# A new plan of the forty slots in the attention and expert phase of one core

## The chip, the core and the metric

The kernel runs on one NeuronCore of a Trainium2 chip, with 16 DMA engines of its own. The metric is the device time of one execution in microseconds. Five engines work side by side, each through its own instruction list in order: TensorE (PE in the profile), VectorE (DVE), ScalarE (ACT), GpSimd (POOL) and SyncE (SP), which here issues all plain transfers. They meet only at semaphores: an instruction whose semaphore isn't there yet holds all that stands behind it on its engine.

## The reference

The input is x (8, 512, 128) and runs through two stages, in float32:

- x + layernorm(A(layernorm(x))), where A is a bidirectional selective state-space layer. The change doesn't touch it.
- x + layernorm(F(layernorm(x))), where F has causal attention with 16 query heads and 4 key/value heads of size 8, rotary embedding, RMS norms, a residual (x2), and a mixture of 8 experts (top 2 of a softmax router; each expert computes w2 (silu(w1 h) * (w3 h)) with 256 hidden columns, weighted by the router), again with a residual.

## The kernel before

The second stage (`ffn_phase`) begins at 1052 us. It handles the 8 batch entries of 512 tokens as a software pipeline. A period b = -2 ... 10 has forty slots t = 0 ... 39, and every engine has a function (`pe_period`, `act_period`, `dve_period`, `pool_period`) whose loop over t writes its instructions out in the order of the slots; nothing plans this at run time. SyncE's `sp_period` is one list per period, without slots. In period b there are at work:

- *front*, batch b+2: layer norm and RMS norm (`dve_in` 0 to 3, with `pool_in_rstd` between 1 and 2; `h` and `hn` are the two results), transpose, projections of q, k, v (`pe_proj` 0 to 3), the rotary products (`dve_rope`) and their sums (`pool_add` 0 for `qf`, 1 for `kf`). q and k are then split into three bf16 parts: `act_part` and `pool_part` in turns, 0 and 1 for q, 2 and 3 for k.
- *att + 1*, batch b+1: the parts go to memory (`sp_parts_out`) and come back spread over partitions, one group of 4 heads at a time (`sp_parts_in` 0 to 3: three q transfers and one k transfer); TensorE computes scores for the row maxima (`pe_max`, from slot 14 on, group g needs its fetch at slots 14, 24, 34 and 4 of the next period), VectorE reduces them (`dve_max`), and `pe_nm`, `act_nm`, `dve_nm`, `sp_max` bring the negative maxima into q's rows.
- *att*, batch b: one tile of scores per slot. TensorE (`pe_st`) fills one of two PSUM buffers, ScalarE takes the exponential twice (`act_exp`, to f16 and to f32), GpSimd computes the rest of the f16 rounding (`pool_split`), and TensorE multiplies by v four slots later (`pe_pv`). After each ten slots a group is done: `act_den` copies the denominators, `dve_og` adds the three parts; both stand ahead of that slot's exponential and maxima.
- *post*, batch b-1: reciprocals of the denominators and the product (`dve_og_fin`, one per slot in slots 5 to 8), output projection (`pe_wo`), residual `x2` (`dve_post`), RMS norm, router (`pe_gate`, 27 steps `dve_gate` at the slots of `GATE_AT`, `pe_count`), and `pool_scatter` in 8 indirect DMAs of tokens into slots by expert (xs).
- *moe*, batch b-2: experts. 15 tiles of 128 tokens in 4 groups q; each group has 5 steps at every other slot (`moe_at`): transpose of `xg`, first product and tanh, second product and gating (twice), and `pe_down`, `act_y` (the copy to `ysb`) and `sp_y` (its store) behind. `sp_w` loads the weights of the expert that each tile belongs to, four tiles of 384 KB at a time, into 8 buffers.
- *end*, batch b-3: `pool_gather` (8 indirect DMAs), weighted sum (`dve_end`), layer norm, output.

TensorE's two buffers for scores let it run at most two tiles ahead of the exponentials (L1303, `exp_done`); the exponential waits for the product with v of six tiles before; `pe_xg` waits for the whole `xg` transfer, `pe_a` for the group's four weights; the first `pool_gather` waits for the stores of all four groups.

## Time and profile before

| | |
|---|---|
| median of 3 runs | 2045.14 us (2045.09 to 2046.9) |
| the profiled execution | 2054.69 us, its span 2052.8 us |
| TensorE busy | 1401.5 us (68%) |
| VectorE busy | 1617.2 us (79%) |
| ScalarE busy | 1134.1 us (55%) |
| GpSimd busy | 1380.8 us (67%) |

The rows below come from that one execution. "Busy" is time inside instructions; a gap in front of an instruction is put down to what released it. L1549 is line 1549 of the kernel; lines are those of the functions above. The span starts at 0; the second stage fills 1052 to 2052.8 us. A period's slot is told here by its first exponential (L1549); the first of batch 4 starts at 1496.66 us.

### The profile page before, as it was taken

How to read it: one execution, taken by the hardware profiler on the slowest of the kernel's cores; microseconds unless marked ns; L12 is line 12 of the kernel's file. 1: busy time of each engine (PE TensorE's matmuls, PEld its weight loads, DVE VectorE, ACT ScalarE, POOL GpSimd, SP SyncE). 2: the span in 40 equal slices, each digit the busy share in tenths (PEclk: the TensorE clock that was granted, in tenths of full speed). 3: DMA queues.
4: the chain of work that ended last, by engine and by line, in shares of the span. 5: the costliest groups of instructions: out<-in, count | busy, mean ns of one | idle time of the engine just before them, and what ended most of it. 6: DMA issues, size and time to landing. Idle time of an engine off the chain costs nothing. (4 is left out here: it accounts for less than half of the span.)

```text
span 2052.8 us, 28868 instructions
## 1 busy us (share of the span) xinstructions
PE 1401.5 (68%) x8048; PEld 986.7 (48%) x8048; DVE 1617.2 (79%) x2570; ACT 1134.1 (55%) x1901; POOL 1380.8 (67%) x1225
## 2 busy tenths in 40 slices
PE   3776666775767767567635877787777787878553
PEld 1444444454534545445422444555555555656453
DVE  2999999999999999999924567586868686866432
ACT  4555665555656545666301877666565666667110
POOL 1776777777777766777742777768686867778333
PEclk9777778887778877778555898899989988999776
DMA  4201222202122102222011112435343524343453
GB/s 161 88 30 55 103 83 103 83 19 85 83 103 83 77 26 83 103 83 98 1 43 43 38 47 79 129 94 153 95 125 97 146 93 139 102 135 117 123 165 93
DMA packets 113886, 184.93 MB, mean 90 GB/s; under 512 B 9856, under 2 KB 86656, under 8 KB 109440
## 3 DMA queue, kind: packets, MB, share of 16 engines
q1 hardware_dynamic: 109664, 175.14, 25.2%
q0 software_dynamic: 4096, 8.40, 1.4%
q8 instruction: 44, 0.72, 0.2%
q14 instruction: 82, 0.67, 0.1%
HBM read 153.03 MB, written 25.89 MB: 87 GB/s over the span
## 5 line engine op out<-in xcount | busy, mean ns | idle before, releaser
L731 POOL TENSOR_TENSOR hc<-hb,cb 128x512 f32<-128x512 f32 x512 | 654.7, 1297 | 247.7 <-DVE hb L610 213.9
L610 DVE TENSOR_TENSOR_SCAN hb<-da,dbu 128x512 f32<-128x512 f32 x512 | 599.9, 1203 | 5.6 <-DVE stats L635 4.0
L499 ACT ACTIVATE da<-dt,a_neg 128x512 f32<-128x512 f32 x512 | 352.2, 718 | 354.8 <-DVE hb L610 303.7
L2041 POOL TENSOR_TENSOR pp<-pt,pp 128x512 f16<-128x512 f32 x320 | 379.0, 1188 | 169.3 <-ACT pt L1550 167.1
L331 PE MATMUL yp<-ident,hc 128*128 128x128 f32 x2048 | 357.9, 317 | 64.9 <-POOL hc L731 64.4
L1689 DVE TENSOR_REDUCE mx<-ms 128x1 f32<-128x384 f32 (+3 forms) x352 | 220.2, 636 | 206.3 <-PE ms L1273 199.4
L331 PEld LDWEIGHTS yp<-ident,hc 128*128 128x128 f32 x2048 | 297.3, 165 | 174.5 <-POOL hc L731 93.9
L603 DVE TENSOR_TENSOR dbu<-dtu,bp 128x512 f32<-128x512 f32 x512 | 324.0, 678 | 2.9 <-PE bp L319 2.2
L1549 ACT ACTIVATE pp<-scores,lift 128x512 f16<-128x512 f32 x320 | 220.3, 688 | 133.4 <-PE scores L1309 128.8
L319 PE MATMUL bp<-st,sel 96*128 96x512 bf16 x256 | 116.7, 456 | 154.3 <-DVE dbu L603 151.7
L1550 ACT ACTIVATE pt<-scores,lift 128x512 f32<-128x512 f32 x320 | 220.3, 688 | 0.0
L1328 PE MATMUL og<-pp,vpad 128*128 128x512 f16 (+3 forms) x1024 | 205.8, 322 | 10.2 <-DVE osum L1710 5.6
L285 PE MATMUL wp<-xpad,wu 128*128 128x512 f32 x256 | 136.8, 627 | 22.8 <-ACT xpad L429 15.4
L1273 PE MATMUL ms<-k,q 72*128 72x384 bf16 (+3 forms) x512 | 139.7, 331 | 0.0
L1328 PEld LDWEIGHTS og<-pp,vpad 128*128 128x128 bf16 x1024 | 105.0, 105 | 66.2 <-issue 26.4
L1309 PE MATMUL scores<-q,k 75*128 75x512 bf16 (+3 forms) x512 | 132.0, 320 | 0.0
L1270 PE MATMUL ms<-mask,identb 128*128 128x128 bf16 (+2 forms) x352 | 93.3, 265 | 49.0 <-issue 17.3
L319 PEld LDWEIGHTS bp<-st,sel 96*128 96x128 bf16 x256 | 25.7, 101 | 210.1 <-DVE dbu L603 188.8
L2060 POOL DMA_INDIRECT yk<-ys_scratch,pos_e x64 | 61.8, 966 | 66.3 <-DMA ys_scratch<-ysb 51.8
L1306 PE MATMUL scores<-mask,identb 128*128 128x256 bf16 (+1 forms) x320 | 85.5, 267 | 25.9 <-ACT pt L1550 24.5
L1394 PE MATMUL pa<-xt,wt 128*128 128x128 f32 x480 | 73.6, 299 | 36.1 <-DVE ga L1845 34.0
L1566 ACT ACTIVATE th<-pa 128x512 f32<-128x512 f32 (+1 forms) x64 | 36.4, 569 | 109.3 <-PE pa L1387 91.1
(193 smaller groups left out, 2351.8 us busy)
## 6 DMA issues: line engine op xcount, KB each, us to landing
cb<-c_scratch SPq DMA_DIRECT2D x16, 3072.0 KB, 11.9
wt<-ffn_w_e SPq DMA_DIRECT2D x120, 384.0 KB, 3.9
cb<-c_scratch SPq DMA_DIRECT2D x16, 1024.0 KB, 4.6
q<-q_scratch SPq DMA_DIRECT2D x96, 96.0 KB
xg<-xs_scratch SPq DMA_DIRECT2D x8, 960.0 KB, 5.6
ys_scratch<-ysb SPq DMA_DIRECT2D x24, 256.0 KB, 2.3
q_scratch<-qp SPq DMA_DIRECT2D x24, 128.0 KB
k<-k_scratch SPq DMA_DIRECT2D x32, 72.0 KB
```

Of the source, the lines that this page charges most:

```text
L319: nc.tensor.matmul(bp[:, n % 2, :], sel[:, n, :], st[:, d, :], start=True, stop=True).then_inc(b_ready, 1)
L331: last = nc.tensor.matmul(yp[:, c, h * P:(h + 1) * P], src[:, c * P:(c + 1) * P], ident[:, :], is_transpose=True, start=(s < 0 and h == 0 ...
L499: nc.scalar.activation(da[:, s % NDA, :], dt[:, d, h, :], ACT.Exp, scale=a_neg[:, d, h, n:n + 1]).then_inc(da_done, 1)
L603: nc.vector.tensor_tensor(dbu[:, s % 2, :], dtu[:, d, h, :], bp[:, n % 2, :], ALU.mult).then_inc(dbu_done, 1)
L610: nc.vector.tensor_tensor_scan(hb[:, s % NHB, :], da[:, s % NDA, :], dbu[:, s % 2, :], 0.0, ALU.mult, ALU.add).then_inc(scan_done, 1)
L731: nc.gpsimd.tensor_tensor(hc[:, s % NHC, :], hb[:, s % NHB, :], cb[:, d, s // 2, :], ALU.mult).then_inc(hc_done, 1)
L1273: last = nc.tensor.matmul(heads[:, i, :], q9[0:PART_ROWS, h0_ + i, c * P:(c + 1) * P], k9[0:PART_ROWS, (h0_ + i) // 4, 0:width], start=Fal ...
L1328: last = nc.tensor.matmul(og[:, kc * P:], vpad[:, kc, h, :], pp[:, (ST_TILES * b + t) % NPR, part, at:at + SEQ - kc * P], start=first, sto ...
L1549: nc.scalar.activation(pp[:, (ST_TILES * b + t) % NPR, 0, 0:width], scores_in, ACT.Exp, bias=lift[:, :], scale=SCALE)
L1550: nc.scalar.activation(pt[:, (ST_TILES * b + t) % NPR, 0:width], scores_in, ACT.Exp, bias=lift[:, :], scale=SCALE).then_inc(exp_done, 1)
L1689: nc.vector.reduce_max(mx[:, c, h:h + n], ms[:, t % 2, 0:n * (c + 1) * P].rearrange("p (n k) -> p n k", n=n), mybir.AxisListType.X).then_i ...
L2041: nc.gpsimd.tensor_tensor(pp[:, (ST_TILES * b + t) % NPR, 1, 0:width], pt[:, (ST_TILES * b + t) % NPR, 0:width], pp[:, (ST_TILES * b + t) ...
```

## The change

Only the order of instructions and some semaphore counts change; each instruction and each transfer is there as before, with the same shape.

- Experts: every step four slots later (slots 6, 8, ... 38 and 0, 2, 4 of the next period), with the second-layer products and the `ysb` copies.
- Post: reciprocals in slots 6, 8, 10, 12, expert steps of VectorE between them in the odd ones; output projection 13 instead of 9, x2 14, its statistics 15 and 16, normalization 16 and 17, router from 22 instead of 20, scatters 32 to 39 instead of 31 to 38.
- Front: VectorE's statistics in slots 0 and 2 instead of 13 and 14, `h` in 18 instead of 24, `hn` in 26 instead of 27; q's projections in 32 and 36, k's in 38, v's in slot 1 of the next period; add q in 38 instead of 34; add k and all of k's parts in the next period.
- End: gathers in 11 to 18 instead of 6 to 13; the weighted sum in two halves.
- Within a slot the exponential stands ahead of `act_den` and the maxima ahead of `dve_og`.
- SyncE: a new order of the period's list. `xg` and the first weights stand near the start of the period in which they are used, after the fetch for group 3, instead of at the end of the period before, where the weights stood ahead of `xg`.

The diff; unchanged lines are left out where it says "...", and the indentation is cut:

```diff
@@ -780,7 +780,7 @@
-GATE_AT = (20, 20, 21, 21, 21, 22, 22, 23, 23, 24, 25, 25, 26, 26, 26, 28, 28, 28, 29, 29, 29, 30, 30, 31, 31, 32, 32)
+GATE_AT = (22, 22, 23, 23, 24, 24, 24, 25, 25, 26, 26, 26, 27, 28, 28, 29, 29, 29, 30, 30, 30, 31, 31, 32, 32, 33, 33)
@@ -810,14 +810,14 @@ moe_at
-    at = (b - 3, MOE_STEPS - 1) if t == 0 else (b - 2, t // 2 - 1)
+    at = (b - 2, t // 2 - 3) if t >= 6 else (b - 3, MOE_STEPS - 3 + t // 2)
...
-for f, at in ((0, 10 * q + 9), (1, 10 * q + 13)):
+for f, at in ((0, 10 * q + 13), (1, 10 * q + 17)):
@@ -827,7 +827,7 @@ down_at, out_at
-at = 10 * q + 14
+at = 10 * q + 18
@@ -1168,54 +1168,53 @@ sp_period
-    if valid(front) and front > 0:
-        sp_xa(sp, front)
...
-    if valid(end):
-        sp_y(sp, end, 3)
+    if valid(moe):
+        sp_xg(sp, moe)
...
+    if valid(end):
+        sp_x2e(sp, end)
+        sp_xr(sp, end)
+    if valid(moe):
+        sp_w(sp, moe, 0)
...
     if valid(end):
-        sp_x2e(sp, end)
-        sp_xr(sp, end)
+        sp_y(sp, end, 3)
...
-    if valid(moe):
-        sp_y(sp, moe, 0)
-        sp_w(sp, moe, 2)
...
+    if valid(moe):
+        sp_w(sp, moe, 2)
+        sp_y(sp, moe, 0)
+    if valid(front):
+        sp_h0(sp, front)
+    if post == 0:
+        sp.wait_ge(consts, 5)
+        sp.dma_start(xs.rearrange("(j p) m -> p j m", p=P), xg[:, :, :]).then_inc(zeroed, 16)
...
     if valid(moe):
+        sp_w(sp, moe, 3)
...
-        sp_w(sp, moe, 3)
+    if valid(front + 1):
+        sp_xa(sp, front + 1)
...
-    if valid(front):
-        sp_h0(sp, front)
...
-    if valid(post):
-        if post == 0:
-            sp.wait_ge(consts, 5)
-            sp.dma_start(xs.rearrange("(j p) m -> p j m", p=P), xg[:, :, :]).then_inc(zeroed, 16)
-        sp_w(sp, post, 0)
+        sp_max(sp, att + 1, 0)
...
-    if valid(att + 1):
-        sp_max(sp, att + 1, 0)
-    if valid(post):
-        sp_xg(sp, post)
@@ -1246,11 +1245,11 @@ pe_proj
+        if valid(b - 1):
+            pe.wait_ge(nm_rem, count(nm_rem, b - 1, 1))
...
-        if valid(b - 1):
-            pe.wait_ge(nm_rem, count(nm_rem, b - 1, 1))
@@ -1279,7 +1278,7 @@ pe_nm
         if valid(b + 1):
-            pe.wait_ge(rope_mul, count(rope_mul, b + 1, 2))
+            pe.wait_ge(rope_mul, count(rope_mul, b + 1, 1))
@@ -1429,26 +1428,28 @@ pe_period
         if valid(post):
-            if t == 9:
+            if t == 13:
                 if post == 0:
...
-            if t == 17:
+            if t == 19:
                 pe_x2t(pe, post)
-            if t == 19:
+            if t == 21:
                 pe_gate(pe, post)
...
+        if t == 1 and valid(att + 1):
+            pe_proj(pe, att + 1, 3)
...
-            if t in (32, 33, 37, 39):
-                pe_proj(pe, front, (32, 33, 37, 39).index(t))
+            if t in (32, 36, 38):
+                pe_proj(pe, front, (32, 36, 38).index(t))
...
-        if t == 35 and valid(att + 1):
+        if t == 34 and valid(att + 1):
             pe_nm(pe, att + 1, 0)
@@ -1538,7 +1539,7 @@ act_part
     else:
-        act.wait_ge(part_pool, count(part_pool, b, k // 2 + 1))
+        act.wait_ge(part_pool, count(part_pool, b, k))
@@ -1589,25 +1590,25 @@ act_period
     for t in range(ST_TILES):
+        if valid(att):
+            act_exp(act, att, t)
+            if t in (14, 24, 34):
+                act_den(act, att, (t - 14) // 10)
...
-        if valid(att):
-            if t in (14, 24, 34):
-                act_den(act, att, (t - 14) // 10)
-            act_exp(act, att, t)
...
         if valid(att + 1):
-            if t in (0, 1):
-                act_part(act, att + 1, (1, 3)[t])
-            if t in (2, 4):
-                act_v(act, att + 1, (t - 2) // 2)
-        if t == 5 and valid(att):
+            if t in (1, 2, 4):
+                act_part(act, att + 1, {1: 1, 2: 2, 4: 3}[t])
+            if t in (3, 5):
+                act_v(act, att + 1, (t - 3) // 2)
+        if t == 6 and valid(att):
             act_vpad(act, att, 3)
         if valid(att + 1):
-            if t == 8:
+            if t == 9:
                 if att + 1 == 0:
@@ -1615,18 +1616,18 @@
-        if valid(att + 1) and t in (35, 36):
-            act_nm(act, att + 1, 0, t - 35)
+        if valid(att + 1) and t in (34, 35):
+            act_nm(act, att + 1, 0, t - 34)
         if valid(post):
-            if t == 18:
+            if t == 20:
                 act_h2t(act, post)
-            if t == 22:
+            if t == 24:
                 act_ex(act, post)
...
-            if t in (36, 39):
-                act_part(act, front, {36: 0, 39: 2}[t])
+            if t == 39:
+                act_part(act, front, 0)
@@ -1853,20 +1854,20 @@ dve_end
-def dve_end(dve, b, k):
+def dve_end(dve, b, k, j=0):
     if k == 0:
...
-        for j in range(TOP):
...
+        if j == 0:
+            dve.wait_ge(gathered, count(gathered, b, 16 * TC * TOP))
+            dve.wait_ge(keep_done, count(keep_done, b, 2))
+            dve.wait_ge(out_done, count(out_done, b, 0))
+            dve.wait_ge(x2e_loaded, count(x2e_loaded, b, 16))
+            dve.wait_ge(end_step, count(end_step, b, 0))
+        for c in range(TC):
+            if j:
+                dve.wait_ge(ye_done, count(ye_done, b, c + 1))
+            nc.vector.scalar_tensor_tensor(ye[:, c, :], yk[:, c, j, :], wn_e[:, c, j:j + 1],
+                                           ye[:, c, :] if j else x2e[:, c, :],
+                                           ALU.mult, ALU.add).then_inc(ye_done, 1)
@@ -1889,53 +1890,56 @@ dve_period
     for t in range(ST_TILES):
+        for f, i in max_at(b, t):
+            dve_max(dve, f, i)
...
-        for f, i in max_at(b, t):
-            dve_max(dve, f, i)
...
         if valid(post):
-            if 5 <= t < 5 + TC:
-                dve_og_fin(dve, post, t - 5)
-            if t == 10:
+            if t in (6, 8, 10, 12):
+                dve_og_fin(dve, post, t // 2 - 3)
+            if t == 14:
                 dve_post(dve, post, 0)
+            if t == 15:
                 dve_post(dve, post, 1)
-            if t == 11:
+            if t == 16:
                 dve.wait_ge(post_step, count(post_step, post, 4))
...
         if valid(front):
-            if t == 13:
+            if t == 0:
                 dve_in(dve, front, 0)
-            if t == 14:
+            if t == 2:
                 dve.wait_ge(in_step, count(in_step, front, 4))
...
-            if t == 24:
+            if t == 18:
                 dve_in(dve, front, 2)
-            if t == 27:
+            if t == 26:
                 dve_in(dve, front, 3)
...
-        if valid(att + 1) and t in (36, 37):
-            dve_nm(dve, att + 1, 0, t - 36)
+        if valid(att + 1) and t in (35, 36):
+            dve_nm(dve, att + 1, 0, t - 35)
         if valid(end):
-            if t in (18, 19):
-                dve_end(dve, end, t - 18)
-            if t == 21:
+            if t in (20, 22):
+                dve_end(dve, end, 0, (t - 20) // 2)
+            if t == 23:
+                dve_end(dve, end, 1)
+            if t == 25:
                 dve.wait_ge(end_step, count(end_step, end, 4))
...
-        if valid(moe) and t in (17, 24):
-            dve_keep(dve, moe, (t - 17) // 7)
+        if valid(moe) and t in (19, 24):
+            dve_keep(dve, moe, (t - 19) // 5)
...
         if valid(front):
-            if t in (32, 34):
-                dve_rope(dve, front, (t - 32) // 2)
-            if t == 38:
+            if t in (33, 37):
+                dve_rope(dve, front, (t - 33) // 4)
+            if t == 39:
                 dve_rope(dve, front, 2)
@@ -1990,12 +1994,12 @@ pool_part
     if k % 2 == 0:
-        pool.wait_ge(part_act, count(part_act, b, 1 if k == 0 else 2))
+        pool.wait_ge(part_act, count(part_act, b, k + 1))
...
     else:
-        pool.wait_ge(part_act, count(part_act, b, 3 if k == 1 else 4))
+        pool.wait_ge(part_act, count(part_act, b, k + 1))
@@ -2067,31 +2071,31 @@ pool_period
         if valid(att + 1):
-            if t in (0, 1, 2):
-                pool_part(pool, att + 1, (2, 1, 3)[t])
-            if t in (3, 5):
-                pool_v(pool, att + 1, (t - 3) // 2)
+            if t == 1:
+                pool_add(pool, att + 1, 1)
+            if t in (0, 2, 3, 5):
+                pool_part(pool, att + 1, {0: 0, 2: 1, 3: 2, 5: 3}[t])
+            if t in (4, 6):
+                pool_v(pool, att + 1, (t - 4) // 2)
         if valid(end):
-            if 6 <= t < 6 + TC * TOP:
-                pool_gather(pool, end, t - 6)
-            if t == 22:
+            if 11 <= t < 11 + TC * TOP:
+                pool_gather(pool, end, t - 11)
+            if t == 26:
                 pool_rstd(pool, end, 2, end_rstd, 0, end_step, 8)
-            if 23 <= t < 26:
-                pool_out(pool, end, t - 23)
+            if 27 <= t < 30:
+                pool_out(pool, end, t - 27)
         if valid(post):
-            if t == 13:
+            if t == 16:
                 pool_rms(pool, post, 1, post_rstd, 0, post_step, 8)
-            if t == 14:
+            if t == 17:
                 pool_h2n(pool, post)
-            if 31 <= t < 31 + TC * TOP:
-                pool_scatter(pool, post, t - 31)
+            if 32 <= t < 32 + TC * TOP:
+                pool_scatter(pool, post, t - 32)
         if valid(front):
-            if t == 16:
+            if t == 3:
                 pool_in_rstd(pool, front)
-            if t in (34, 38):
-                pool_add(pool, front, (t - 34) // 4)
-            if t == 36:
-                pool_part(pool, front, 0)
+            if t == 38:
+                pool_add(pool, front, 0)
```

## Rows read from the trace of the kernel before

**Rows 1.** Busy time by window, one per batch of attention, the last the tail; columns: window, length, busy (instructions) per engine, clock, DMA.
```profile
1496.66:1606.02 109.36, 84.25 (x586) 62.01 (x586) 79.56 (x158) 67.77 (x129) 81.39 (x78) 0.89 0.39 118
...
1714.14:1808.51 94.37, 77.29 (x549) 57.09 (x550) 72.88 (x135) 66.11 (x125) 70.97 (x69) 0.89 0.43 129
1808.51:1893.79 85.28, 67.00 (x489) 51.07 (x487) 54.47 (x107) 59.67 (x106) 66.97 (x62) 0.90 0.41 124
1893.79:2052.80 159.01, 77.09 (x445) 67.95 (x443) 54.19 (x140) 16.66 (x32) 56.12 (x61) 0.74 0.41 124
```

**Rows 2.** Busy time by window, batch 4 in four parts (A, B, C, D).
```profile
1496.66:1532.86 36.20, 26.13 (x176) 19.11 (x176) 23.62 (x45) 24.66 (x47) 28.51 (x28) 0.86 0.54 159
1532.86:1572.52 39.66, 31.01 (x212) 23.52 (x213) 30.60 (x68) 22.32 (x43) 26.72 (x28) 0.83 0.35 109
1572.52:1580.83 8.31, 7.44 (x61) 5.83 (x61) 7.45 (x19) 6.01 (x11) 4.73 (x5) 1.00 0.12 40
1580.83:1606.02 25.19, 19.66 (x139) 13.53 (x139) 17.88 (x28) 14.78 (x30) 21.44 (x20) 1.00 0.32 98
```

**Rows 3.** Waits, 1496.66 to 1606.02: who waited for whom, us in total, times, longest.
```profile
ACT kp L1539 <- POOL kf L1986: 11.2, 2, 5.6
...
PE pa L1394 <- DVE ga L1845: 5.5, 1, 5.5
...
PE ms L1270 <- DMA k<-k_scratch: 3.4, 2, 3.3
...
PE pa L1377 <- DMA xg<-xs_scratch: 3.1, 1, 3.1
```

**Rows 4.** Timeline of SyncE's issues: start, us, queue, line, transfer.
```profile
1510.34 0.36 SPq L1162 DMA_DIRECT2D ys_scratch<-ysb  x1
...
1511.80 0.63 SPq L1105 DMA_DIRECT2D q_scratch<-qp  x1
...
1516.99 3.77 SPq L1152 DMA_DIRECT2D wt<-ffn_w_e  x4
...
1524.18 0.68 SPq L1118 DMA_DIRECT2D k<-k_scratch  x1
```

**Rows 5.** Timelines of SyncE and TensorE, at batch 0's first maxima and in batch 4.
```profile
1093.14 0.68 SPq L1118 DMA_DIRECT2D k<-k_scratch  x1
...
1098.97 0.59 PE L1270 MATMUL ms<-mask,identb 128*128 128x512 bf16 x1 [17.30 <-issue]
...
1532.86 0.39 PE L1270 MATMUL ms<-mask,identb 128*128 128x512 bf16 x1 [3.26 <-DMA k<-k_scratch]
```

**Rows 6.** Timeline of GpSimd, the sum for k ahead of batch 4.
```profile
1494.81 1.28 POOL L1986 TENSOR_TENSOR kf<-rotk 32x512 f32<-32x512 f32 x1
```

**Rows 7.** Groups of instructions, 1496.66 to 1606.02: busy us, mean ns, idle before.
```profile
L2041 POOL TENSOR_TENSOR pp<-pt,pp 128x512 f16<-128x512 f32 x41 | 49.4, 1206 | 24.8 <-ACT pt L1550 24.5
...
L2050 POOL DMA_INDIRECT xs_scratch<-h2n,posi x8 | 8.3, 1038 | 1.3 <-issue 1.3
...
L1651 DVE TENSOR_SCALAR h<-xa,mv,ln_r 128x128 f32<-128x128 f32 x4 | 4.2, 1115 | 0.0
...
L1966 POOL TENSOR_TENSOR ln_r<-ln_var,mhalf 128x8 f32<-128x8 f32 x1 | 1.6, 1637 | 0.1
```

**Rows 8.** One line's instructions, 1400 to 1700 us: duration in ns, min/median/max.
```profile
L1651 DVE TENSOR_SCALAR hn<-xa,mv,ln_r x12: 333/336/1106, 1462.9 to 1681.9; 128x128 f32<-128x128 f32 x12
```

**Rows 9.** Waits in batch 7 (1808.51 to 1893.79) and groups in batch 1 (1200 to 1290).
```profile
PE pa L1377 <- DMA xg<-xs_scratch: 7.0, 1, 7.0
...
L2050 POOL DMA_INDIRECT xs_scratch<-h2n,posi x8 | 8.4, 1050 | 5.5 <-DMA xs_scratch<-xg 4.4 <-issue 1.2
```

**Rows 10.** Timelines of SyncE and TensorE in the tail.
```profile
1971.11 0.38 SPq L1142 DMA_DIRECT2D xg<-xs_scratch  x1
...
1976.75 1.11 PE L1377 MATMUL pa<-ident,xg 128*128 128x128 f32 x4 [9.81 <-DMA xg<-xs_scratch]
...
1978.93 1.85 PE L1387 MATMUL pa<-xt,wt 128*128 128x128 f32 x8
```

11 lines of the change are left out of this document (removed).

## The prediction

> **What bounds the kernel now.** I first cut the trace into batches of attention, from one first exponential of slot 0 to the next [rows 1]. The change touches nothing ahead of 1052 us. A full batch (there are three, batches 3 to 5, within 1.3 us of each other; I work on the middle one, whose row stands) takes 109.4 us. In it no engine is full: TensorE is busy 84 us, VectorE 80, GpSimd 81, ScalarE 68. So the forty slots run from wait to wait, and the question is which waits end last. The batch without a front (6) takes 94, the one without a next batch (7) 85, and after the last exponential 159 us remain.
>
> Then I cut the middle batch in four [rows 2]: A, from slot 0 to the end of TensorE's wait in slot 14 (36.2 us); B, to slot 28 (39.7); C, to slot 32 (8.3); D, to the next slot 0 (25.2). The list of waits [rows 3] names what stands at the cuts: ScalarE waits 5.6 us twice (two batch starts lie in the window) for `kf`, TensorE 3.1 us for the `xg` transfer in slot 2, 3.3 us for `k` in slot 14 and 5.5 us for `ga` in slot 26. In D GpSimd is busy 21.4 of 25.2 us, in B VectorE 30.6 of 39.7 with the `ga` wait in its middle, in A nothing is near full: A is a chain of SyncE. SyncE starts k's and q's parts outward at 1511.80, after the store of slot 4's `ysb` (1510.34) on which it waited, then four expert weights (1516.99), then fetches q and k for group 0, the last of them issued at 1524.18 [rows 4], and TensorE goes on at 1532.86 [rows 5], 8.0 us after that issue ended.
>
> **The change part by part.**
> *D and the batch's seam.* Before, GpSimd holds three extra operations in slots 34 to 38 (add q, first remainder of q, add k) beside the scatters, and ScalarE stands at slot 39 until add k ends (1494.81 + 1.28 = 1496.1 [rows 6]), so slot 0's exponential starts at 1496.66. After, only add q stays, in slot 38, and ScalarE's copy after exponential 39 waits for that. GpSimd's work from slot 32 through this add: 7 splits of 1.21 us and 7 scatters of 1.04 + 0.16 (the row's 1.3 us idle over 8) [rows 7] = 16.8, plus 1.3 = 18.1 us. ScalarE's exponentials ahead of it and its copy behind it, 1.9 (a little over the 1.7 that its 67.8 us make per slot [rows 1]), make D 20.0 us: 5.2 less. GpSimd is the bound here, so the wait on `kf` becomes a shorter wait on `qf`, of 2 to 4 us. Below: if GpSimd has a backlog at slot 32, D stays at 23. TensorE's waits on the rope products go, since the projections now stand at 32, 36 and 38; that is inside the 5.2.
>
> *A.* The `xg` transfer is needed in slot 6 instead of 2, and its 3.1 us go; the reciprocals stand in every other slot; neither is worth anything by itself, since A ends with the k transfer. That chain now begins later: from the end of add q, GpSimd has slot 39 (2.4), slot 0 with q's first remainder (2.4), slot 1 with add k (2.5), slot 2 (2.4), slot 3 with k's remainder and the new normalization's power (1.2 + 1.2 + 1.64 + 0.5 = 4.5), slot 4 (1.7), slot 5 with k's third part (2.4) = 18.3 us, 17.7 after the exponential of slot 0. Before it was SyncE's wait for `ysb` that set 15.1. Behind it: from the start of the parts to the end of the last fetch's issue 13.1 us [rows 4], less 1.0 for the two loads that now go ahead, plus 0.5 for the store of the last `ysb` that now goes behind the weights: 12.5. Then 8.0 of landing. A = 17.8 + 12.5 + 8.0 = 38.3 us, 2.1 more. The upper bound is 41 (the first weights, 1.5 MB, are now also issued in slots 1 to 4, and could slow the parts); the lower is 33: the same fetch landed 5.2 us after its issue with no weights ahead of it (1093.14 + 0.68 to 1098.97 [rows 5]), and GpSimd may be 2.5 us earlier. What was bought in D is partly paid here.
> The `ysb` store of the last group now lies behind the parts and the weights; the gathers, from slot 11, wait for it on GpSimd with the splits queued behind them. It lands about 28 to 33 us after slot 0, in time for the splits that TensorE needs after slot 14, so I cost it at nothing in A.
>
> *B.* VectorE's work is only moved. The normalization `h` (four operations, 4.2 us [rows 7]) goes from slot 24 to 18, where VectorE has gaps, while two router steps and half of the end's sum come in from slots below 20: slots 20 to 27 lose about 1.5 us of work net; x2, its statistics and their aggregation (1.9) come into B from slots 10 and 11. The `ga` wait of 5.5 us should fall to 2; against that the second layer norm's GpSimd steps stand at slots 16 and 17 beside gathers (about 7.5 us in two slots) and may delay `h2n` for slot 19 by 1 to 2 us. I take B at 37.7, 2.0 less (bounds 35 and 42). C is VectorE's and stays.
> In both places two of VectorE's operations are long beside GpSimd: `h` has a mean of 1.12 us [rows 7], `hn`, the same operation and shape, a median of 0.34 with single ones of 1.11 [rows 8]. In the new plan `hn` stands in slot 26, just where GpSimd has the end's `rstd` and `yo`, which earlier had stood beside `h`.
> The Trainium skill, page "SBUF — State Buffer", section "Who interferes with whom", says that a two-port VectorE operation and a GpSimd operation exclude each other, the later waiting for the whole of the earlier. By that rule nothing shrinks with the move of `h` and `hn` grows; the rows agree in that no other reason for 0.34 against 1.12 is seen.
>
> *A full batch* then takes 38.3 + 37.7 + 8.3 + 20.0 = 104.3 us against 109.4: 5 less.
>
> *All batches.* Batches 3 to 5: 15. Batch 2 (its first fourteen slots are shorter, so A costs one more): 4. Batch 1: as in D, and the scatters no longer wait 4.4 us for the zeroing [rows 9], which goes out 15 slots earlier but then lies ahead of one q and k fetch: 5. Batch 0: 1. Batch 6 has no front (D was short already): 0. Batch 7 has no k chain: the wait on `xg`, 7.0 us there [rows 9], goes, less 1 for the later scatter: 6.
> *Tail.* Two more expert steps are left when attention ends, but TensorE stands about as long for `xg` (9.8 us at 1976.75 [rows 10]) and they fill it. The first weights, though, were issued before `xg` and now follow it and three more loads: `xg` issued at 1971.11, TensorE needs the weights at 1978.93, 7.8 us later; 2.3 us to the first weight's issue, 3.8 for four, 4 to land give 10 to 11. That is 3 us in the last round and 2 in the one before. And batch 6's last `ysb` store follows four or eight weights, so the gathers and the sum that VectorE does ahead of the next `ga` are 2 us later: in all 7 more.
> Sum: 15 + 4 + 5 + 1 + 0 + 6 - 7 = 24 us. The profiled execution took 2054.7 us around a span of 2052.8, 9.6 above the median of 2045.1; taken off it gives 2031, off the median 2021.
>
> **The rivals.**
> 1. *GpSimd keeps pace and the k fetch lands early* (the lower bounds): A 33, B 36, D 20, so 97.5, 12 less in four batches (48), 7 in batch 1, 1 + 3 + 6, less 7: 58, 1987 us. For it: GpSimd is idle for 28 us of the batch. Against: its work is dense just in slots 32 to 5. Chance 0.20.
> 2. *VectorE is blocked longer*: `hn` takes 4.2 instead of 1.9, and B is 40 or 41 instead of 37.7. The gain is 2.7 per batch, about 13 in all: 2032 us. It is what the page's rule gives. Chance 0.15.
> 3. *The seam's gain is spent in slot 14*: the k chain costs 5 us more, D gains 5: no change but for batch 7 and the tail, 2045 us. Chance 0.09.
> 4. *Slower: k's transfer comes too late.* A goes to 41 and more because the added weights ahead of the parts share the 16 DMA engines, and D stays at 23 since GpSimd carries a backlog from the gathers: 41 + 39.7 + 8.3 + 23 = 112, 2.6 more in five batches, with the tail's 7 and the 11 of batches 1 and 7 about 9 more: 2054. It decides from k's third part more than 20 us after slot 0's exponential. Chance 0.15.
> My forecast has the rest, 0.41.
>
> **How the numbers follow.** Forecast 2021. The range of 8 in 10 goes from 1993, within rival 1, to 2048, within rival 4. Differences under 0.2% (4.1 us) can't be told from none here. Faster: 0.41 + 0.20 + 0.15 = 0.76; same 0.09; slower 0.15.
>
> **What would show it.** Right: in a full batch the wait of ScalarE on `kf` is gone and one on `qf` of 2 to 4 us stands before slot 0; no wait on `xg` in slots 2 or 6; TensorE's wait on the k transfer in slot 14 grows from 3.3 to 5 to 9 us, and stands 38 us after slot 0; the `ga` wait of slot 26 is under 3 us; in the tail waits on the weights of 2 to 3 us. Wrong: slot 14 without a wait (rival 1), `hn` at 1 us each (rival 2), full batches of 109 us or more (3, 4), or waits at new places, as at the gathers' slot 11 or the `og` sums that now follow the exponential.

## The result and the profile after

The changed kernel takes 2098.77 us (2096.98 to 2101.36) against 2046.02 in the same comparison: ratio 1.0245, interval 1.0205 to 1.0285. It is slower by 50 us (the ratio's 2.45%) where 24 fewer were forecast, and outside the range.

First the windows of the changed kernel, the same cuts as in [rows 1]: batches 0, 1, 2, 4, 6, 7 and the tail, each with its length, the busy time of TensorE (its matmuls, then its weight loads), VectorE, ScalarE and GpSimd with the number of instructions, and behind them the granted clock of TensorE as a share of 2.4 GHz, the busy share of the DMA engines and GB/s.

```profile
1136.58:1218.75 82.17, 63.99 (x368) 36.88 (x366) 43.89 (x79) 59.58 (x112) 55.49 (x51) 0.79 0.09 29
1218.75:1315.37 96.62, 69.79 (x401) 40.77 (x400) 64.26 (x126) 62.57 (x116) 66.41 (x65) 0.79 0.16 49
1315.37:1418.70 103.33, 78.79 (x557) 56.14 (x557) 70.16 (x138) 69.56 (x128) 66.71 (x65) 0.92 0.35 109
1528.53:1635.47 106.94, 84.43 (x588) 61.40 (x587) 73.52 (x160) 69.19 (x128) 78.91 (x78) 0.90 0.39 121
1743.10:1844.60 101.50, 79.48 (x564) 59.35 (x564) 67.05 (x138) 67.31 (x126) 72.58 (x71) 0.90 0.38 117
1844.60:1938.90 94.30, 71.30 (x485) 53.37 (x482) 54.84 (x107) 60.87 (x107) 67.62 (x65) 0.87 0.36 113
1938.90:2099.30 160.40, 80.99 (x459) 72.62 (x459) 53.47 (x142) 17.15 (x33) 53.43 (x58) 0.72 0.44 134
```

Lengths by batch (from one first exponential to the next, in us), with the experiments that the argument needs; "start" is the first exponential of batch 0:

| kernel | start | 0 | 1 | 2 | 3 | 4 | 5 | 6 | 7 | tail |
|---|---|---|---|---|---|---|---|---|---|---|
| before | 1130.4 | 70.0 | 89.3 | 98.4 | 108.6 | 109.4 | 108.1 | 94.4 | 85.3 | 159.0 |
| after | 1136.6 | 82.2 | 96.6 | 103.3 | 109.9 | 106.9 | 107.6 | 101.6 | 94.2 | 160.4 |
| e10 | 1132.3 | 69.2 | 89.8 | 99.2 | 102.9 | 104.7 | 105.2 | 96.6 | 90.4 | 160.4 |
| e13 | 1133.4 | 76.5 | 92.7 | 98.4 | 102.4 | 102.4 | 102.8 | 101.8 | 90.8 | 152.5 |
| e15 | 1132.0 | 69.4 | 89.9 | 98.9 | 106.1 | 103.8 | 100.6 | 92.5 | 90.2 | 160.9 |

Of the 46.5 us between the two spans, 6.2 lie ahead of batch 0, 24.4 in batches 0 to 2, 7.2 in batch 6, 8.9 in batch 7, 1.4 in the tail; the full batches give back 1.7 together. I worked on the full batch; the loss sits nearly all outside it. Against the forecast, batches 0 to 2 are 34 us too long, batch 7 is 15, the full ones together 13, batch 6 is 7, the time ahead of batch 0 is 6, and the tail is 6 us shorter than forecast.

The clock column says something that the lengths don't. Here are batches 0 and 1 of the kernel before, the same two of e10 (an experiment below, without the late parts), and two stretches of batch 0 in the changed kernel:

```profile
1130.40:1200.40 70.00, 57.38 (x364) 33.56 (x362) 42.63 (x75) 59.59 (x112) 55.44 (x51) 0.88 0.12 37
1200.40:1289.70 89.30, 64.34 (x396) 38.32 (x394) 63.88 (x121) 61.90 (x117) 67.66 (x66) 0.85 0.21 65
```
```profile
1132.32:1201.50 69.18, 57.53 (x364) 33.09 (x363) 41.89 (x77) 58.99 (x112) 54.67 (x51) 0.88 0.12 38
1201.50:1291.30 89.80, 69.69 (x396) 41.63 (x394) 59.55 (x124) 62.23 (x117) 65.95 (x65) 0.79 0.17 52
```
```profile
1163.60:1170.40 6.80, 4.22 (x18) 2.11 (x19) 2.65 (x4) 1.86 (x4) 1.16 (x2) 0.50 0.05 17
1184.20:1194.30 10.10, 7.37 (x32) 4.27 (x33) 4.68 (x7) 3.24 (x6) 2.53 (x3) 0.50 0.03 9
```

In batch 0 the mean clock falls from 0.88 to 0.79, and about the same matmuls keep TensorE busy for 64.0 us instead of 57.4. Worked out from these means, it stood at the lower level (1.2 GHz) for some 34 us instead of 17. Two of the stretches at 0.50 begin while TensorE stands in its two waits on k (shown below) and go on for 4.6 and 8.6 us behind them. In e10's batch 0, where those waits are 1.6 us each, clock and busy time are back. So a long wait there comes with slower matmuls behind it; how much of the 12.2 us is the wait and how much the clock is not told apart. The clock alone doesn't set a batch's length: e10's batch 1 has 0.79 too and 69.7 us busy, and takes 89.8 us, as before.

The waits of the changed kernel in its batch 4 (who waited for whom, us, times, longest), answering to [rows 3]:

```profile
DVE pos_e L1829 <- DMA yk<-ys_scratch,pos_e: 7.0, 1, 7.0
...
PE ms L1269 <- DMA k<-k_scratch: 5.2, 2, 3.8
PE og L1327 <- DVE osum L1711: 4.7, 3, 2.9
POOL yk L2064 <- DMA ys_scratch<-ysb: 4.2, 1, 4.2
...
PE m L1351 <- POOL h2n L2013: 3.6, 1, 3.6
ACT qp L1540 <- POOL qf L1990: 3.5, 2, 1.8
...
PE m L1239 <- DVE slot_of L1799: 2.6, 1, 2.6
```

The `kf` wait has become one of 1.8 us on `qf`, the `xg` wait is gone, `ga` holds TensorE 0.7 us in all: three announced effects came. But five waits are new or have grown from under half a microsecond, on the gathers (`pos_e`), `osum`, the `ysb` store, `h2n` and `slot_of`, and the two on k have grown from 3.4 to 5.2 us together.

SyncE at the start of batch 0 and before it, with the answering waits of TensorE (start, us; in brackets the idle time and what ended it):

```profile
1104.70 0.38 SPq L1082 DMA_DIRECT2D h_scratch<-h  x1
1105.19 2.13 SPq L1115 DMA_DIRECT2D q<-q_scratch  x3
1107.36 0.68 SPq L1118 DMA_DIRECT2D k<-k_scratch  x1
...
1152.91 0.60 SPq L1105 DMA_DIRECT2D q_scratch<-qp  x1
...
1160.63 0.68 SPq L1118 DMA_DIRECT2D k<-k_scratch  x1
```
```profile
1112.99 0.61 PE L1269 MATMUL ms<-mask,identb 128*128 128x512 bf16 x1 [4.97 <-DMA k<-k_scratch]
...
1165.80 0.61 PE L1269 MATMUL ms<-mask,identb 128*128 128x512 bf16 x1 [5.06 <-DMA k<-k_scratch]
...
1185.70 0.61 PE L1269 MATMUL ms<-mask,identb 128*128 128x512 bf16 x1 [3.97 <-DMA k<-k_scratch]
```

The first fetch for group 1 was issued at 1093.93 before and at 1105.19 now: the new list has the store of `h` ahead of it, and that kept SyncE waiting for VectorE's slot 18, 10.1 us. The parts leave at 1152.91, 16.3 us after exponential 0; before, at 1138.49, 8.1 after it. In batch 0 TensorE waits 9.0 us for k in all, 1.5 before; there is no expert work in batches 0 and 1 (before, the first transpose of `xg` runs at 1294.8) to fill the time until k lands.

### The profile page after: what moved, and what is told of

It reads as the page before. It is cut to its first block and busy times, and to the rows that moved or that the text cites. A ratio compares the mean times of both kernels' runs of the same rounds, so it can differ in the third digit from the quotient of the medians.

```text
span 2099.3 us, 28868 instructions
## 1 busy us (share of the span) xinstructions
PE 1428.2 (68%) x8048; PEld 1002.9 (48%) x8048; DVE 1592.8 (76%) x2570; ACT 1141.9 (54%) x1901; POOL 1367.6 (65%) x1225
## 5 line engine op out<-in xcount | busy, mean ns | idle before, releaser
L2045 POOL TENSOR_TENSOR pp<-pt,pp 128x512 f16<-128x512 f32 x320 | 371.6, 1164 | 206.0 <-ACT pt L1551 204.5
L1327 PE MATMUL og<-pp,vpad 128*128 128x512 f16 (+3 forms) x1024 | 213.2, 332 | 33.5 <-DVE osum L1711 28.9
L1308 PE MATMUL scores<-q,k 75*128 75x512 bf16 (+3 forms) x512 | 137.0, 331 | 0.0
L1305 PE MATMUL scores<-mask,identb 128*128 128x256 bf16 (+1 forms) x320 | 88.0, 275 | 17.9 <-ACT pt L1551 17.8
```

Of the source, the lines that this page charges most:

```text
L1308: last = nc.tensor.matmul(sp_[:, t % 2, at:at + SEQ - kc * P], k9[:, h // 4, kc * P:(kc + 1) * P], q9[:, h, kc * P:], start=False, stop=Tr ...
L1327: last = nc.tensor.matmul(og[:, kc * P:], vpad[:, kc, h, :], pp[:, (ST_TILES * b + t) % NPR, part, at:at + SEQ - kc * P], start=first, sto ...
L2045: nc.gpsimd.tensor_tensor(pp[:, (ST_TILES * b + t) % NPR, 1, 0:width], pt[:, (ST_TILES * b + t) % NPR, 0:width], pp[:, (ST_TILES * b + t) ...
```

## The experiments

Ratios are to the kernel before, run in the same comparison, with the 95% interval. "Parts early" stands for the whole block of q's and k's projections, rope, adds, remainders, v and `nm`'s first half (the negative maxima), at the slots of the kernel before. The kernel before had medians of 2046 to 2057 us in the six comparisons, and the changed kernel stood in the first alone, beside four runs of the kernel before. So the steps from it to e1, e5, e6 and e9 are less sure than those between later experiments, beside which the kernel before ran 13 to 35 times.

**e1_parts_early** (changed kernel, parts early), **e4_before_parts_late** (kernel before, parts late):

```diff
-                    if t in (32, 36, 38):
-                        pe_proj(pe, front, (32, 36, 38).index(t))
+                    if t in (32, 33, 37, 39):
+                        pe_proj(pe, front, (32, 33, 37, 39).index(t))
...
-            if t in (0, 2, 3, 5):
-                pool_part(pool, att + 1, {0: 0, 2: 1, 3: 2, 5: 3}[t])
+            if t in (0, 1, 2):
+                pool_part(pool, att + 1, (2, 1, 3)[t])
```

> The changed kernel with one block put back as before: projections, rotary products, sums and the three parts of q, k and v, and the row maxima's transposes of the first half, on all engines. Theory 1 (k's third part now comes in slot 5 of the next period and the fetch of q and k for slot 14 with it): the first exponential of batch 0 stays at 1136.6 us, batch 0 falls from 82 to about 74 us, batches 1, 2 and 6 by 4 to 6 each, in all 25 to 30 us less than the changed kernel, near 2071. Theory 2 (SyncE's new list holds the fetches back behind transfers that wait for other work): less than 8 us, near 2093, because the fetch of group 1 still stands behind the store of h.

> The kernel before with the one block as in the changed kernel (projections, rotary products, parts of q, k, v and the first half's transposes), all else as before. Theory 1: 20 to 28 us slower than before, near 2070, batch 0 about 8 us longer with a wait on the k transfer in slot 14 of 4 us or more. Theory 2: within 8 us of before, near 2050.

e1: 1.0133 (1.0070 to 1.0196), so about 23 us come back; batch 0 falls from 82.2 to 76.9. e4: 1.0021 (0.9994 to 1.0048). Over all the same block has a price on the changed kernel and hardly one on the kernel before. But e4's batch 0 is longer too, 74.7 against 70.0, with a wait on k of 5.5 us in slot 14: what theory 1 said of that place came, and an earlier start (1128.7) and a shorter tail (156.1) gave it back in that profile.

**e2_old_sync_list**, **e3_parts_early_old_list**: SyncE's list as before, under the new slots, without and with e1's edit (the list's diff is the one of `sp_period` above, reversed).

> The changed kernel with SyncE's list of a period as before, all slots as changed. Theory 2: the first exponential of batch 0 back at 1130.4 us, the wait in slot 24 of batch 0 gone, the gathers' wait in slot 11 gone, batch 7 some 6 us shorter; 20 to 25 us less than the changed kernel, near 2076. Theory 1: at most the 6 us of the start, near 2093, because k's parts are late whatever stands around their stores.

> Both of the last two: the block of parts and SyncE's list as before; what stays of the change are the experts four slots later, the reciprocals in turns, VectorE's and GpSimd's other moves, and the order of exponential and group sums. If theories 1 and 2 together are the whole cause: 2046 us or a little under, as the kernel before. If the rest costs too: above 2055.

1.0821 (1.0768 to 1.0873) and 1.0839 (1.0786 to 1.0891). The old list has the last `ysb` store behind its first fetch, and that `ysb` is now made in slot 8; all behind it waits. A full batch takes 134 to 139 us. The list is not a part that can be judged alone: it belongs to the experts' slots, and the two runs decide nothing between the theories.

**e5_h_store_after_fetch**, **e6_end_sum_later**:

```diff
+            if valid(att + 1):
+                sp_parts_in(sp, att + 1, 1)
             if valid(front):
                 sp_h0(sp, front)
...
-            if valid(att + 1):
-                sp_parts_in(sp, att + 1, 1)
```

(and the load of the next input likewise behind the fetch for group 2)

```diff
-                    if t in (20, 22):
-                        dve_end(dve, end, 0, (t - 20) // 2)
+                    if t in (22, 23):
+                        dve_end(dve, end, 0, t - 22)
...
-                if valid(moe) and t in (19, 24):
+                if valid(moe) and t in (22, 24):
```

> The changed kernel with two moves in SyncE's list: the store of h (which waits for VectorE's slot 18) and the next load of x1 now stand behind the fetches of groups 1 and 2 instead of ahead of them. If the list's order costs by these (theory 2): first exponential of batch 0 back from 1136.6 to about 1131, batches 0 and 1 each 3 to 5 us shorter, full batches 1 to 2; 12 to 18 us less than the changed kernel, near 2083. If the late parts alone set slots 14 and 24 (theory 1): only the 5 us of the start.

> The changed kernel with VectorE's end work two slots later: the copy of the positions from slot 19 to 22, the halves of the weighted sum in 22 and 23, their statistics in 24. Theory 3 (gathers in slots 11 to 18, with their landing, end after VectorE needs them in slot 19, where it waits 7 to 8 us): that wait goes, and as VectorE's work is moved and not more, 3 to 5 us are won in each of the batches 3 to 7: 15 to 22 us, near 2080. Rival: TensorE's wait for h2n in the same slot (3.6 us) ends nearly as late, and next to nothing is won: 2095.

1.0188 (1.0141 to 1.0235) and 1.0191 (1.0144 to 1.0237): some 11 us each, but both intervals overlap the changed kernel's (from 1.0205), so neither step is shown by itself. e5 brings the start back from 1136.6 to 1132.4, four of its us; e6 shortens batch 0 too (80.2), where nothing of its edit acts, so not all of its 11 us can be its own; 6.2 more of them lie in the tail. In the full batches e6 gains next to nothing (107.8 against 108.1): VectorE's wait on `pos_e` is gone, TensorE's on `h2n` stays at 3.6 us and ends last, which was the rival.

**e7_early_h_end** (e1, e5 and e6 together) and **e8_and_gate29** (also router steps 18 and 19 in slot 29 instead of 30):

```diff
-GATE_AT = (22, 22, 23, 23, 24, 24, 24, 25, 25, 26, 26, 26, 27, 28, 28, 29, 29, 29, 30, 30, 30, 31, 31, 32, 32, 33, 33)
+GATE_AT = (22, 22, 23, 23, 24, 24, 24, 25, 25, 26, 26, 26, 27, 28, 28, 29, 29, 29, 29, 29, 30, 31, 31, 32, 32, 33, 33)
```

> The three together: the block of parts early (as in e1_parts_early), the store of h behind the fetches, the end's sum two slots later. If the three theories name the whole loss and add up: 2098.8 - 23 - 15 - 18 = 2043, at or under the kernel before. If they overlap: 2055 to 2065.

> As e7_early_h_end, and router step 19 in slot 29 instead of 30, as it stood before, so that TensorE's transpose of hn in slot 30 no longer waits 2.6 us for it: 2 to 4 us less in each of the batches 1 to 5, 10 to 15 us under e7_early_h_end. Rival: VectorE's work in slots 29 and 30 is the same sum, and the wait moves to slot 29's maxima: 0.

1.0075 (1.0050 to 1.0099) and 1.0054 (1.0028 to 1.0081). The intervals overlap: the step of e8 is not shown. Nor did its mechanism come. In batch 4 TensorE's transposition in slot 30 still waits 2.29 us for router step 19 (2.63 in e7), and slots 28 to 31 still take 10.7 us (10.6 in e7, 8.3 before).

**e9_group_sums_first** (changed kernel), **e10_all_but_experts** (e8 and this), **e11_before_sums_last** (kernel before with the reverse):

```diff
-                for f, i in max_at(b, t):
-                    dve_max(dve, f, i)
                 if t == 4 and valid(post):
                     dve_og(dve, post, NKV - 1)
...
+                for f, i in max_at(b, t):
+                    dve_max(dve, f, i)
```

(and ScalarE's copy of the denominators likewise ahead of the slot's exponential)

> The changed kernel, with only the order inside slots 4, 14, 24 and 34 as before: ScalarE copies the group's denominators ahead of the slot's exponential, and VectorE makes the group's output sums ahead of the slot's maxima (which wait for TensorE's scores, and those for the k fetch). Theory: in the changed kernel TensorE waits for these sums at every group boundary, 4.7 us three times over in a full batch and 1 to 3 us more per boundary in batch 0, so that the order costs about 3 us in each of eight batches: the time falls by 15 to 25 us below the changed kernel's, to about 1.015 of the kernel before, and the waits of TensorE on osum go. Rival: the wait only moves to the maxima that now stand behind the sums, or to the k fetch: under 5 us, 1.022 or more.

> The changed kernel with the four edits put together: k's and q's parts early as before, h0's store and the load of the next input behind the fetches of k, the end's sum two or three slots later, the gate's steps 18 and 19 in slot 29, and the order of sums, denominators, maxima and exponential as before. Left of the change are the experts four slots later and the SyncE list that goes with them. Theory (the order costs about 15 us): 10 to 20 us under the same kernel without the order, which took 1.0054 of the kernel before: 0.996 to 1.000. Rival (order worth nothing): 1.003 to 1.007.

> The kernel before, with only the order of the change: exponential ahead of the denominators' copy, maxima ahead of the output sums. Theory: slower by 10 to 20 us, 1.005 to 1.010, and TensorE's waits on osum appear at slots 4, 14, 24 and 34. Rival: under 4 us, within 0.2%, since the sums then wait behind maxima for which TensorE has its scores ready.

e9: 1.0185 (1.0135 to 1.0235), 12 us, less than expected, and its interval overlaps the changed kernel's. e10: 0.9992 (0.9970 to 1.0015), 13 us under e8, the intervals apart, and level with the kernel before. e11: 1.0014 (0.9996 to 1.0032), which misses the 10 to 20 us: the order alone costs nothing measurable on the kernel before. How it can cost is in VectorE's timeline of the changed kernel at batch 0's slot 24; second, the kernel before, with the old order:

```profile
1186.78 0.69 DVE L1690 TENSOR_REDUCE mx<-ms 128x4 f32<-128x512 f32 x1 [4.77 <-PE ms L1272]
1187.50 0.68 DVE L1709 TENSOR_TENSOR osum<-osum,og 32x512 f32<-32x512 f32 x1
1188.21 0.68 DVE L1711 TENSOR_TENSOR osum<-osum,og 32x512 f32<-32x512 f32 x1
```
```profile
1168.10 0.68 DVE L1708 TENSOR_TENSOR osum<-osum,og 32x512 f32<-32x512 f32 x1 [0.52 <-ACT osum L1509]
1168.81 0.68 DVE L1710 TENSOR_TENSOR osum<-osum,og 32x512 f32<-32x512 f32 x1
1169.52 0.69 DVE L1689 TENSOR_REDUCE mx<-ms 128x4 f32<-128x512 f32 x1
```

In the first the sums stand behind a maximum that waits 4.77 us for k; TensorE, which needs the sums for the next outputs, then waits for them (1189.14, 1.23 us). In the second they wait for nothing but their input.

That e11 costs nothing is a sum of two sides. Its batches 0, 1, 2 and 7 are longer by 3.3, 2.0, 2.2 and 4.2 us, and its full ones shorter by 3.9 on average. There the four operations of `h` behind the sums take 1.1 us instead of 4.2, and TensorE's wait on `ga` in slot 26 is gone (batch 4, the kernel before and e11):

```profile
1560.51 4.22 DVE L1651 TENSOR_SCALAR h<-xa,mv,ln_r 128x128 f32<-128x128 f32 x4
```
```profile
1563.99 1.11 DVE L1651 TENSOR_SCALAR h<-xa,mv,ln_r 128x128 f32<-128x128 f32 x4
```

So the new order has a gain that the prediction didn't count either; that `h` is the whole of it is not shown.

**e12_parts_late_rest_undone**: as e10, with the parts late as in the change.

> As e10_all_but_experts, but with k's and q's parts in the next period, as in the change. If the parts in the next period cost here what they cost when they alone were moved on the kernel before (about 4 us), this is 0.2% above e10; if they cost what their undoing gave back on the changed kernel (about 20 us), 1%. The changed order of the parts has its price in the first fourteen slots of batches 0 and 1.

1.0107 (1.0073 to 1.0142): 1.15% above e10, 23 us, the second of the two prices foretold.

**e13_before_parts_late_sums_last**: the kernel before with parts late and sums last together, experts and list untouched.

> The kernel before with two parts of the change together, without the experts' shift and without the new SyncE list: k's and q's parts in the next period, and the order of the change (exponential ahead of denominators, maxima ahead of output sums). Alone on the kernel before they took 1.0021 and 1.0014. Theory A (each edit has a price only where the moved experts have taken the slack that hides it): together 1.002 to 1.005. Rival B (the two harm each other through the k fetch, since VectorE's maxima wait for k and the sums stand behind them): 1.010 or more.

1.0011 (0.9993 to 1.0030): theory A. The two don't harm each other, and the whole program pays for them only with the rest of the change in place. What they do in the full batches the cuts show (means of batches 3 to 5, in us, from the first exponential of one slot to that of the next):

| kernel | slots 0-14 | 15-27 | 28-31 | 32-39 | sum |
|---|---|---|---|---|---|
| before | 38.6 | 36.6 | 8.3 | 25.2 | 108.7 |
| e4 (parts late) | 42.8 | 36.8 | 8.3 | 21.2 | 109.1 |
| e11 (sums last) | 39.6 | 31.6 | 8.3 | 25.3 | 104.8 |
| e13 (both) | 40.9 | 32.0 | 8.3 | 21.2 | 102.5 |
| e10 (experts, list) | 32.7 | 36.5 | 10.6 | 24.5 | 104.3 |
| e12 (e10, parts late) | 38.9 | 35.0 | 10.8 | 21.2 | 106.0 |
| after | 38.8 | 36.8 | 11.4 | 21.2 | 108.1 |

Parts late take 3.0 to 4.1 us out of slots 32 to 39 in every kernel. They put 4.2 into slots 0 to 14 on the kernel before (e4) and 6.2 on the shifted one (e12 against e10), where that stretch was six us shorter and k's chain now fills it (in batch 5 TensorE waits 4.7 us for k in slot 14, 2.6 in e10). That is a difference of some 2 us in each of three batches. More of the 23 us lies in batches 0 to 2: 13.8 in e12 against e10, 5.5 in e4 against the kernel before. In e13 batches 0, 1, 6 and 7 lose 6.5, 3.4, 7.4 and 5.5 us as in the changed kernel, and the full batches, with the tail, pay for that; in the changed kernel they don't.

**e14_last_store_and_norm_earlier**, **e15_first_weights_earlier**, **e16_both** (all on e10):

```diff
+                sp_y(sp, end, 3)
+            if valid(moe):
                 sp_w(sp, moe, 1)
-            if valid(end):
-                sp_y(sp, end, 3)
...
-                    if t == 17:
+                    if t == 16:
                         pool_h2n(pool, post)
```
```diff
-                sp_w(sp, moe, 0)
...
                 sp_max(sp, att + 1, 0)
+            if valid(post):
+                sp_w(sp, post, 0)
```

(in e14 with the statistics and the power ahead of `h2n` one slot earlier too)

> As e10_all_but_experts, and the last ysb store stands ahead of the second four weights instead of behind them, and the second layer norm's statistics, power and h2n stand one slot earlier. Theory: the gathers' wait on this store (2.4 us in a full batch) goes, pos_e's wait in slot 19 and TensorE's on h2n (3.6 to 5.8 us in slot 19) shrink to 1 to 2 us, and 2 to 3 us go per batch in six batches: 12 to 18 us under e10, 0.991 to 0.994 of the kernel before. Rival: slot 22 to 30 is filled by VectorE and takes the gain back: under 4 us.

> As e10_all_but_experts, with the first four expert weights issued at the end of the period before, ahead of xg, as in the kernel before. Theory: TensorE's waits on wt in batch 7 (2.8 us at slot 8) and three times in the tail (4.3 to 4.6 us of the chain each) go: 6 to 10 us under e10. Rival: xg then lands later by the weights' 3.7 us of issue, and TensorE waits for xg instead: within 3 us of e10.

> e14_last_store_and_norm_earlier and e15_first_weights_earlier together. If both theories hold, 18 to 28 us under e10, 0.986 to 0.991 of the kernel before, and so faster than both kernels; if both rivals hold, 0.997 to 1.001.

e14: 1.0019 (0.9998 to 1.0040), e15: 0.9960 (0.9945 to 0.9976), e16: 0.9987 (0.9969 to 1.0005). e15 came out as expected, 0.3% under e10 with intervals that just overlap, and is the first version under both kernels. But the gain isn't where the theory put it. The waits on the weights did go, and in batch 7 one of 7.6 us on k (slot 4) came, in the tail longer ones on `h2n` and `ga`: batch 7 and tail take 251.1 us together against 250.8 in e10. What is shorter in the profile are batches 5 and 6 (100.6 and 92.5 against 105.2 and 96.6), in batch 5 with the waits on k of slots 14 and 24 (2.6 and 2.0 us) gone. Why is not shown. e16, at 0.9987, fell into the range of both rivals. e14 missed: slot 19 of its batch 4 falls from 5.0 to 1.4 us, but slot 20 grows from 2.7 to 6.9. VectorE and, under it, GpSimd in that stretch of e14:

```profile
1535.82 5.17 DVE L1651 TENSOR_SCALAR h<-xa,mv,ln_r 128x128 f32<-128x128 f32 x4
1540.93 0.54 DVE L1689 TENSOR_REDUCE mx<-ms 128x1 f32<-128x384 f32 x1
1541.39 0.67 DVE L1845 SCALAR_TENSOR_TENSOR ga<-th,pa 128x512 f32<-128x512 f32 x1
```
```profile
1536.35 1.05 POOL L2011 TENSOR_TENSOR h2n<-x,rt 128x512 f32<-128x512 f32 x1
1537.35 1.17 POOL L2043 TENSOR_TENSOR pp<-pt,pp 128x512 f16<-128x512 f32 x1
1538.67 1.06 POOL L2062 DMA_INDIRECT yk<-ys_scratch,pos_e  x1 [0.16 <-issue]
1539.75 1.16 POOL L2043 TENSOR_TENSOR pp<-pt,pp 128x512 f16<-128x512 f32 x1
```

The four operations of `h` take 5.2 us, with GpSimd at work without a pause, and TensorE waits 3.1 us for the `ga` behind them. In e10 the same four took 1.1 us.

**e17_both_h_at_9** (e16) and **e18_weights_h_at_9** (e15), with `h` in slot 9:

```diff
-                    if t == 18:
+                    if t == 9:
                         dve_in(dve, front, 2)
```

> As e16_both, with the four operations of h in slot 9 instead of 18. In e14 and e16 h takes 5.2 and 4.0 us in slot 18, where GpSimd's gathers and splits run without a stop, against 1.1 us in e10 and in the changed kernel, where GpSimd stands at its statistics. Theory: it is this that took back the gain of e14; in slot 9, beside splits alone, h takes under 2.5 us, at a place where VectorE has gaps, and the kernel falls 8 to 15 us below e16, to 0.992 to 0.995 of the kernel before. Rival: h stays at 4 us there, or the gain goes to another wait (k in slot 14): within 4 us of e16.

> As e15_first_weights_earlier, with h in slot 9. There h had its 1.1 us at slot 18, hidden behind TensorE's wait on h2n. Theory: nothing to win, within 4 us of e15 (0.994 to 0.998 of the kernel before). Rival: h's place costs in slot 18 too: 5 us or more under e15.

e17: 0.9950 (0.9929 to 0.9971), 0.4% under e16, with intervals that just meet. e18: 1.0022 (1.0007 to 1.0037), 0.6% above e15: neither theory. In both, `h` takes 2.9 us in slot 9 in full batches. That is less than the 4.0 of e16's batch 4 and more than the 1.1 of e15, which fits both signs; that it is the whole cause is not shown, and the profiles don't bear it out: e17's batch 4 takes 109.3 us with 2.9 for `h`, e16's 103.5 with 4.0. In e17's batch 4 the bound has moved on to k, whose fetch for group 1 stands behind a `ysb` store, on which SyncE waits 6.6 us for the gathers:

```profile
1550.36 0.39 SPq L1162 DMA_DIRECT2D ys_scratch<-ysb  x1
1550.84 2.33 SPq L1115 DMA_DIRECT2D q<-q_scratch  x3
1553.21 0.68 SPq L1118 DMA_DIRECT2D k<-k_scratch  x1
```
```profile
1558.92 0.61 PE L1270 MATMUL ms<-mask,identb 128*128 128x512 bf16 x1 [8.07 <-DMA k<-k_scratch]
```

e15 and e17 are the fastest; which of the two is faster isn't settled.

## Why the prediction was wrong

The step that failed is the one from the full batch to all batches: the late parts were priced where expert work stands beside them (2 us against 5 won in D), and batches 0, 1 and 6, where little or nothing does, were put at -1, -5 and 0. With it went the order of maxima and sums, put at nothing. The runs showed +12.2, +7.3 and +7.2 in those batches, 23 us for the late parts over the whole program (e12 against e10) and 13 for the order (e10 against e8). The full batch itself came out 2.6 us too long (106.9 against 104.3). Part by part:

- **D and the seam** (25.2 to 20.0 forecast): right. With the same cut D takes 21.0 and the `qf` wait is 1.8 us, a little under the 2 to 4 announced.

```profile
1528.53:1563.72 35.19, 25.96 (x181) 18.77 (x181) 21.40 (x38) 25.87 (x49) 27.22 (x28) 0.89 0.60 183
1563.72:1603.01 39.29, 30.66 (x215) 23.05 (x215) 29.20 (x75) 22.00 (x41) 26.47 (x28) 0.88 0.27 83
1603.01:1614.44 11.43, 8.26 (x55) 5.90 (x54) 7.62 (x17) 6.50 (x11) 7.67 (x8) 0.85 0.62 189
1614.44:1635.47 21.03, 19.56 (x141) 13.68 (x139) 15.30 (x31) 14.82 (x27) 17.55 (x17) 1.00 0.15 49
```

- **A** (38.3): 35.2, 3.1 less. The parts left 16.8 us after slot 0 instead of 17.8, the 12.5 to the end of the last fetch's issue came as worked out, and k landed 5.9 us behind it, not 8.0: the landing was the term too large. The wait on k in slot 14 is 3.8 us against 3.3 in [rows 3], not 5 to 9, and stands 35 us after slot 0, not 38. What I missed is the other side: without the late parts A would have been shorter still (slots 0 to 14: 32.7 in e10, 38.8 after), so the rest of the change, the experts' shift with its list above all, whose `xg` wait I priced at nothing, was worth 6 us there, and the late k chain spent them. Which of its edits was is not shown.
- **B** (37.7): 39.3. The `ga` wait went as forecast, and in its place came TensorE's 3.6 us on `h2n` in slot 19. GpSimd makes `h2n` between gathers, and the first of them waits 4.2 us for the last `ysb` store. "I cost it at nothing" was checked against the splits behind the gathers, not against the normalization. VectorE's 7.0 us on `pos_e` in the same slot look worse than they are: e6 takes them away, and the full batches stay as long.
- **C** ("stays", 8.3): 11.4. The transposition of slot 30 waits 2.6 us for router step 19, 0.4 before. The new table has that step one slot later, but this isn't the cause: with it back in slot 29 the wait is still 2.3 us (e8, e10) and the stretch 10.6 to 10.7. Without the experts' shift and the rest that e10 keeps it is 8.3 (e4, e11, e13). Which part lengthens it stays open; that C "stays" was said without a row behind it.
- **Batches 0 and 1** (-1 and -5 forecast): +12.2 and +7.3. This is the step that failed most. They have no expert steps to hide anything, TensorE waits 9.0 us for k in batch 0, and its clock is down for twice as long: batch 0 is back at 69 to 70 us only when parts and order are both as before (76.9 in e1, 75.8 in e9, 75.0 in e12, 69.2 in e10). A price found in the full batch was carried over to batches whose cover is other work.
- **Ahead of batch 0** (nothing): +6.2. Most of it is the store of `h` in SyncE's list; e5 takes 4.2 of it away. The list was read for the gathers and the weights, not for each fetch that now stands behind a store.
- **Batch 6** (0) and **7** (-6): +7.2 and +8.9. Batch 6 has no front, so D had nothing to gain, but the parts of batch 7 are late in it all the same: e1 takes 5.9 back, e4 and e13 lose 3.6 and 7.4 there. The forecast left A's price out of it. In batch 7 the `xg` wait did go, and TensorE's stop on the weights came in its place, with the last `ysb` store behind eight weight loads:

```profile
1857.77 8.68 SPq L1152 DMA_DIRECT2D wt<-ffn_w_e  x8
1869.45 0.39 SPq L1162 DMA_DIRECT2D ys_scratch<-ysb  x1
```
```profile
1866.53 1.87 PE L1386 MATMUL pa<-xt,wt 128*128 128x128 f32 x8 [4.56 <-DMA wt<-ffn_w_e]
```

- **Tail** (+7): +1.4 in this profile, and 149 to 164 us among the kernels with the shift, too wide to judge. The two waits on the weights came, 4.3 and 3.3 us where 2 to 3 were announced.
- **The rivals.** Rival 4 had the sign and the mechanism (k too late), but its place was wrong, not the full batch but the first ones, and its size too (2054). Rival 2 fell: `hn` stays at 0.33 us each, and `h` fell to 0.34 in full batches from 1.12, though the prediction had expected nothing to shrink. The order of maxima and sums, named only in the last sentence and priced at nothing, is worth 12 to 13 us on the changed kernel.

In all, 23 us are the late parts (e10 to e12), about 13 the order (e8 to e10), the rest, some 14, the list's store, the end's sum and perhaps the router's table, not told apart one by one. What e10 keeps of the change (the experts' shift with its list, and the moves of post, front and end) is neutral as a whole, and with one move of the list it pays 0.4% (e15).

## What to carry to other kernels

Price a move in the batch with the least other work as well as in the steady one: the late parts made batch 0 longer by 5 to 6 us on either kernel (e4, e1, e12), and the full one by 0.4 to 3.4. Look at the granted clock beside each new wait. For each step moved later, walk to its last reader and to every entry behind it in its engine's own order, and subtract only once what two edits both take away. An edit that was free on the kernel before can have a price once another has used up its slack, so it has to be tried on both.

## What was not expected of the hardware

The same VectorE operation (`h`, 128x128 f32 in and out) took 0.34 us in full batches of the changed kernel and 1.3 us on average beside GpSimd's splits and gathers (e14); single ones reached 3.0 us (e16). Here is `h` in the changed kernel's batch 4, and GpSimd beside it:

```profile
1574.59 1.11 DVE L1652 TENSOR_SCALAR h<-xa,mv,ln_r 128x128 f32<-128x128 f32 x4
```
```profile
1574.74 0.25 POOL L1981 TENSOR_TENSOR rt<-rt,eps 128x4 f32<-128x4 f32 x1
1575.06 1.06 POOL L1983 TENSOR_TENSOR rt<-rt,mhalf 128x4 f32<-128x4 f32 x1
```

The power of 128x4 elements runs for 1.06 us beside them, and none of the four is longer for it. By the Trainium skill, page "SBUF — State Buffer", section "Who interferes with whom", the port pair that VectorE and GpSimd share is an exclusive lock. The 5.2 us of e14 agree with it: the first `h` operation there ends 0.1 us after the split beside it. But beside this power operation the last two of the four take 0.34 us each as well. So here a GpSimd instruction did not hold the port for as long as it lasts in the profile, whose GpSimd times are rough.
